# Row gathers of an expert stage issued two pairs ahead, each of four row buffers with its own landing semaphores

## The chip, the cores and the metric

One core of one Trainium2 chip. The metric is the device time of one execution in microseconds (us); the median of several runs is given. The engines are called TensorE (PE in the profile; PEld is its weight load), VectorE (DVE), ScalarE (ACT), GpSimd (POOL) and SyncE (SP).

## The reference, cut to what matters

A model of two layers on 16 sequences of 548 tokens (36 image patches and 512 text rows, width 128): a gated attention, a first mixture of experts, a spiking attention and a second mixture of experts. The change lies in the first mixture of experts, in which each of 32 experts chooses 256 of the 8,768 tokens:

```python
k = min(int(bs * C_CAP) // E, bs)
xf = x.reshape(bs, H)
h = xf @ W_router + b_router
Sm = jax.nn.softmax(h, axis=-1)
G_ek, idx_ek = jax.lax.top_k(Sm.T, k)
tokens = xf[idx_ek]
tok_g = tokens.reshape(NUM_GROUPS, GROUP_SIZE, k, H)
up = jnp.einsum('gjkh,ghf->gjkf', tok_g, W_up) + b_up[:, None, None, :]
act = jax.nn.silu(up).reshape(E, k, D_FF)
Eout = jnp.einsum('ekf,efh->ekh', act, W_down) + b_down[:, None, :]
weighted = G_ek[..., None] * Eout
y = jnp.zeros((bs, H), dtype=x.dtype).at[idx_ek.reshape(-1)].add(weighted.reshape(-1, H))
```

bs is 16 x 548 = 8,768, so k is 274; the width of a hidden row (D_FF) is 341.

## The kernel before, in words

The kernel runs its stages one after the other, each in blocks of its own; a block's engines all finish before the next block begins. The stage of the change is `run_experts` (L1036). Ahead of it `choose_tokens` writes for each expert a list of 320 slots (40 blocks of 8, with room for those that stay empty) to HBM and brings it back as row numbers: `slot_tokens` (`gather_idx`) and `slot_sums` (`scatter_idx`). Behind it `add_rows` (L1190) reads the two copies of the sums from HBM and adds them to the residual H.

The 32 experts are worked in 16 pairs. A pair q has 2 x 320 = 640 slots, five tiles of 128 rows (PTILES = 5); expert o = 0 of the pair owns the first two and a half tiles, o = 1 the rest.

**GpSimd** issues all indirect DMAs. `gather(q)` issues five of them (L1083), each of 128 token rows of 160 floats into `rows[q % 4]`, one of four row buffers. `scatter(q)` issues five (L1092) that add 128 result rows each from `y[q % 2]` to the sums in HBM; ahead of them it waits until the scatter of pair q - 1 has landed (`added`, L1088 to L1089) and hands a y buffer back (`y_free`), and each of the five waits for its y tile (`y_out`, L1091): the first two need expert 0 of the pair, the other three need expert 1. The order on GpSimd is gather(0), then for each q: gather(q + 1), scatter(q).

**TensorE** turns rows (`turn`, L1107: a transpose of each tile, L1113, behind a wait for the gathers of three tiles, `first_in`, or of the last two, `second_in`), multiplies by the up weights (`project_up`, L1122) and by the down weights (`project_down`, L1133, the bias at L1134). The order is written out by hand: turn(q, second part), project_down(q, 0), project_up(q, 1), turn(q + 1, first part), project_down(q, 1), project_up(q + 1, 0), and so on. In particular project_down(q, 1), the last work of pair q, stands behind the wait for the rows of pair q + 1.

**ScalarE** copies the turned rows out of PSUM (L1166, L1168) and applies Silu (L1174). **VectorE** multiplies the down results by the routing weights that came with the rows, and writes y (L1187), behind a wait for `y_done` from TensorE and for `y_free`. **SyncE** loads the up and down weights (L1073, L1076) as TensorE frees their buffers.

Both gathers of neighbouring pairs count on landing semaphores chosen by q % 2, two of them for the first three tiles and two for the last two; TensorE waits for 48 and 32 more at each second pair.

## Time and profile before

| what | value |
|---|---|
| median of 3 runs | 2144.09 us (2139.62 to 2151.6) |
| profiled execution, its own time | 2146.77 us |
| its span, first to last instruction | 2144.9 us |
| PE busy | 1558.1 us (73%) |
| DVE busy | 1316.5 us (61%) |
| ACT busy | 745.3 us (35%) |
| POOL busy | 720.1 us (34%) |
| mean granted TensorE clock | 0.858 of full speed |
| first gather (L1083) to last scatter (L1092) starts | 815.0 to 1094.2 us |

The shares are means over all stages; the stage of the change takes about an eighth of the span. Register, branch, semaphore and DMA-issuing instructions are not counted as busy, except that the indirect DMAs of GpSimd have a duration of their own in the profile, the time in which GpSimd makes their descriptors. "Idle before" is the time in which an engine did nothing before an instruction, with what ended it; "issue" means that the profile shows nothing that it waited for.

### The profile page before, as it was taken

The page shows a single profiled execution, that of the slowest core. Times are in us where ns is not written, and L with a number is a line of the kernel's source. Part 1 is how long each engine was busy: PE and PEld are TensorE (multiplying, and loading weights), DVE is VectorE, ACT ScalarE, POOL GpSimd, SP SyncE. Part 2 cuts the span into 40 slices and gives each one's busy share as a digit, 9 for nine tenths or more (in the row PEclk, how much of TensorE's full clock was granted, in tenths as well). Part 3 has the DMA queues.
Part 4 walks back from the last instruction along what each step waited for, and adds up shares of the span by engine and source line. Part 5 has one row for each costly group of instructions (what it writes and reads, how often), then busy time and mean ns, then how long its engine had stood idle before and what let it go on. Part 6 is the DMA issues. An engine that isn't in the chain of part 4 may idle for free. (4 is left out here: it accounts for less than half of the span.)

```text
span 2144.9 us, 31340 instructions
## 1 busy us (share of the span) xinstructions
PE 1558.1 (73%) x9132; PEld 1091.4 (51%) x9132; DVE 1316.5 (61%) x2105; ACT 745.3 (35%) x1369; POOL 720.1 (34%) x758
## 2 busy tenths in 40 slices
PE   5679999998601006766647548888888758999998
PEld 3457777775301004555534333333333456888787
DVE  3845555555477891111115777877777547989988
ACT  2245555554200002222203346667766321111111
POOL 1345555552000015777754012322221112323322
PEclk8689999999855556888767889999999858999999
DMA  4050000000210002444352000000000000000000
GB/s 136 0 230 1 0 0 0 0 0 0 84 21 0 1 0 60 73 68 77 70 120 66 4 2 2 0 0 0 0 0 0 1 32 7 12 11 15 11 15 14
DMA packets 69696, 60.85 MB, mean 28 GB/s; under 512 B 15789, under 2 KB 63675, under 8 KB 68363
## 3 DMA queue, kind: packets, MB, share of 16 engines
q1 hardware_dynamic: 52174, 47.52, 7.0%
q0 software_dynamic: 15744, 11.85, 3.9%
q10 hardware_dynamic: 1728, 0.85, 0.1%
q8 instruction: 27, 0.44, 0.1%
q14 instruction: 23, 0.19, 0.0%
HBM read 35.06 MB, written 25.18 MB: 28 GB/s over the span
## 5 line engine op out<-in xcount | busy, mean ns | idle before, releaser
L1609 DVE TENSOR_SCALAR at_clip<-at_slot 128x548 bf16<-128x548 f32 (+1 forms) x320 | 226.3, 722 | 79.0 <-PE at_slot L1452 72.2
L1540 ACT ACTIVATE at_clip<-at_slot,at_four 128x548 bf16<-128x548 f32 (+1 forms) x320 | 226.6, 713 | 126.3 <-PE at_slot L1452 124.5
L1452 PE MATMUL at_slot<-at_qm,at_ks 128*128 128x274 bf16 (+1 forms) x1280 | 216.4, 285 | 55.5 <-ACT at_clip L1540 45.4
L1590 POOL TENSOR_SCALAR at_qm<-at_qs,at_headmask 128x548 bf16<-128x548 bf16 x128 | 97.3, 780 | 359.5 <-DVE at_qs L1618 359.5
L1187 DVE TENSOR_SCALAR ex_y<-ex_ps_y,ex_rows 128x128 f32<-128x128 f32 (+1 forms) x96 | 29.2, 346 | 246.5 <-PE ex_ps_y L1134 246.0
L1452 PEld LDWEIGHTS at_slot<-at_qm,at_ks 128*128 128x128 bf16 (+1 forms) x1280 | 90.5, 97 | 150.3 <-ACT at_clip L1540 90.7
L1092 POOL DMA_INDIRECT moe_sums<-ex_y,slot_sums x80 | 125.0, 1563 | 54.4 <-DVE ex_y L1187 32.6
L467 PE MATMUL ga_kv<-ga_kern,ga_v 128*128 128x274 f32 x512 | 132.1, 400 | 14.8 <-ACT ga_kern L552 14.1
L2041 DVE TENSOR_REDUCE mx_routed<-mx_weighted 128x128 f32<-128x1024 f32 x69 | 137.6, 1994 | 2.4
L612 POOL TENSOR_TENSOR ga_rot<-ga_by_cos,ga_by_sin 128x274 f32<-128x274 f32 (+1 forms) x96 | 70.3, 732 | 165.7 <-DVE ga_by_sin L656 165.7
L1133 PE MATMUL ex_ps_y<-ex_down,ex_hid 128*128 128x128 f32 (+3 forms) x576 | 114.1, 357 | 12.5 <-ACT ex_hid L1174 12.5
L80 PE MATMUL mx_e<-ff_expert_out_high,mx_h_E 128*128 128x512 f32 x276 | 110.2, 399 | 10.9 <-DVE mx_weighted L2038 10.8
L467 PEld LDWEIGHTS ga_kv<-ga_kern,ga_v 128*128 128x128 f32 x512 | 92.5, 189 | 40.0 <-ACT ga_kern L552 18.2
L546 ACT ACTIVATE ga_rot<-ga_rot 128x274 f32<-128x274 f32 (+1 forms) x192 | 79.0, 429 | 96.4 <-POOL ga_rot L612 76.6
L1133 PEld LDWEIGHTS ex_ps_y<-ex_down,ex_hid 128*128 128x128 f32 (+3 forms) x576 | 94.6, 230 | 29.8 <-ACT ex_hid L1174 17.2
L82 PE MATMUL mx_e<-ff_expert_out_high,mx_h_E 128*128 128x512 f32 x276 | 108.4, 393 | 0.0
L81 PE MATMUL mx_e<-ff_expert_out_low,mx_h_E 128*128 128x512 f32 x276 | 108.4, 393 | 0.0
L2000 POOL TENSOR_TENSOR mx_h_E<-mx_hid_E,mx_h_E 128x768 fp32r<-128x768 f32 x23 | 43.4, 1885 | 185.5 <-DVE mx_h_E L2031 185.5
L126 PE MATMUL ln_centred<-H,center_sb 128*128 (+1 forms) x256 | 89.3, 483 | 20.7 <-ACTq L168 10.3
L2038 DVE TENSOR_TENSOR mx_weighted<-mx_e,ff_comb 128x512 f32<-128x512 f32 x138 | 88.7, 682 | 9.8 <-PE mx_e L82 6.5
L227 DVE RECIPROCAL ln_rstd<-ln_rstd 128x548 f32<-128x548 f32 x20 | 71.4, 3572 | 34.9 <-ACT ln_rstd L186 34.9
L1974 ACT ACTIVATE mx_silu_E<-mx_a 128x768 f32<-128x768 f32 x23 | 18.7, 814 | 211.8 <-PE mx_b L82 211.8
(346 smaller groups left out, 3798.4 us busy)
## 6 DMA issues: line engine op xcount, KB each, us to landing
moe_sums<-ga_zeros SPq DMA_DIRECT2D x8, 1152.0 KB, 18.9
ar_rows<-moe_sums SPq DMA_DIRECT2D x32, 256.0 KB
ex_down<-in_down SPq DMA_DIRECT2D x32, 192.0 KB, 2.4
out_h<-H SPq DMA_DIRECT2D x22, 192.0 KB, 1.9
H<-in_text SPq DMA_DIRECT2D x1, 4096.0 KB, 20.7
token_rows<-tr_rows SPq DMA_DIRECT2D x16, 256.0 KB
patches<-in_patches SPq DMA_DIRECT2D x1, 1728.0 KB, 7.6
ga_sin<-in_sin SPq DMA_DIRECT2D x1, 1644.0 KB, 10.1
```

The source lines that it names most:

```text
L80: nc.tensor.matmul(out, weights[0], moving[0], start=start, stop=False)
L81: nc.tensor.matmul(out, weights[0], moving[1], start=False, stop=False)
L82: return nc.tensor.matmul(out, weights[1], moving[0], start=False, stop=stop)
L126: nc.tensor.matmul(xc_ps[j][:, 0:HALF], k["center"][:], tokens(H, i, g, j), start=True, stop=True).then_inc(centred, 1)
L467: last = nc.tensor.matmul(kv[:, e, 0:HALF], v[p][:, mt + 2 * side, e * P:(e + 1) * P], kern[g % 2][:, side, :], start=mt == 0 and side == ...
L1092: nc.gpsimd.indirect_dma_start(out=sums, out_offset=bass.IndirectOffsetOnAxis(ap=scatter_idx[:, t, q:q + 1], axis=0), in_=y[q % 2][:, t, : ...
L1133: nc.tensor.matmul(out, hid[o][0:m, f, s0:s0 + n], down[o][0:m, f, :], start=f == 0, stop=False)
L1452: last = nc.tensor.matmul(slot[SLOT[T % 2][u]][0:rows_of(t), s, 0:HALF], ks[p][:, t * P:t * P + rows_of(t)], qm[p][:, h, j * HALF:(j + 1) ...
L1540: nc.scalar.activation(clip[T % 2][u][0:r], slot[SLOT[T % 2][u]][0:r, :, 0:HALF], ACT.Relu, bias=four[0:r], scale=-1.0).then_inc(by_act, 1)
L1590: last = nc.gpsimd.tensor_scalar(qm[p][:, h, :], qs[:], headmask[:, h:h + 1], 1.0, ALU.mult, ALU.mult)
L1609: nc.vector.tensor_scalar(clip[T % 2][u][0:r], slot[SLOT[T % 2][u]][0:r, :, 0:HALF], 4.0, None, ALU.min).then_inc(by_dve, 1)
L2041: nc.vector.tensor_reduce(R[p][t][:], weighted[:].rearrange("p e d -> p d e"), AX.X, ALU.add).then_inc(reduced, 1)
```

## The change

GpSimd issues gather(0) and gather(1) first, and then for each pair q: gather(q + 2), scatter(q). The landing semaphores are four and four, one pair of them for each row buffer (q % 4), and TensorE's counts follow (the fourth part of q in place of the half). The number of DMAs, their sizes, the four row buffers, the two y buffers and TensorE's own order stay as they were.

```diff
@@ -1054,7 +1054,7 @@
-        first_in, second_in = ([sem(f"{n}{p}") for p in range(2)] for n in ("first_in", "second_in"))
+        first_in, second_in = ([sem(f"{n}{p}") for p in range(4)] for n in ("first_in", "second_in"))
@@ -1081,7 +1081,7 @@
-                                                 in_offset=bass.IndirectOffsetOnAxis(ap=gather_idx[:, t, q:q + 1], axis=0)).then_inc(landed[q % 2], 16)
+                                                 in_offset=bass.IndirectOffsetOnAxis(ap=gather_idx[:, t, q:q + 1], axis=0)).then_inc(landed[q % 4], 16)
@@ -1094,9 +1094,10 @@
             gather(0)
+            gather(1)
             for q in range(PAIRS):
-                if q + 1 < PAIRS:
-                    gather(q + 1)
+                if q + 2 < PAIRS:
+                    gather(q + 2)
                 scatter(q)
@@ -1105,9 +1106,9 @@
-                    pe.wait_ge(first_in[r % 2], 48 * nth + 48)
+                    pe.wait_ge(first_in[r], 48 * nth + 48)
                 else:
-                    pe.wait_ge(second_in[r % 2], 32 * nth + 32)
+                    pe.wait_ge(second_in[r], 32 * nth + 32)
@@ -1140,12 +1141,12 @@
             for q in range(PAIRS):
-                turn(q, q % 4, 1, q // 2)
+                turn(q, q % 4, 1, q // 4)
                 project_down(q, 0)
                 project_up(q, 1, q % 2, q // 2 % 2, q // STEP)
                 if q + 1 < PAIRS:
                     n = q + 1
-                    turn(n, n % 4, 0, n // 2)
+                    turn(n, n % 4, 0, n // 4)
```

## Rows read from the trace of the kernel before

**Rows 1.** The page: the span, and one group of its part 5.
```profile
span 2144.9 us, 31340 instructions
...
L1092 POOL DMA_INDIRECT moe_sums<-ex_y,slot_sums x80 | 125.0, 1563 | 54.4 <-DVE ex_y L1187 32.6
```

**Rows 2.** Busy time by stretch (start:end, length; then each engine's busy time, TensorE's clock, DMA).
```profile
845.30:1084.60 239.30, 168.44 (x828) 129.53 (x827) 25.56 (x84) 61.80 (x119) 177.24 (x140) 0.80 0.40 71
...
1096.00:1107.00 11.00, 0.00 (x0) 0.00 (x0) 0.00 (x0) 0.00 (x0) 0.24 (x1) 0.50 0.33 81
```

**Rows 3.** Waits, 815 to 1100 us: engine, line <- releaser: us, times, longest us.
```profile
PE ex_ps_xt L1113 <- DMA ex_rows<-token_rows,slot_tokens: 67.6, 15, 7.4
...
POOL moe_sums L1092 <- DVE ex_y L1187: 32.6, 16, 5.6
...
POOL moe_sums L1092 <- DMA moe_sums<-ex_y,slot_sums: 2.5, 1, 2.5
```

**Rows 4.** Timeline of POOL (start us, us, engine, line, ...), one pair: gathers, then scatters.
```profile
879.50 1.01 POOL L1083 DMA_INDIRECT ex_rows<-token_rows,slot_tokens  x1 [0.30 <-issue]
...
885.85 1.61 POOL L1092 DMA_INDIRECT moe_sums<-ex_y,slot_sums  x1 [0.30 <-issue]
887.77 1.56 POOL L1092 DMA_INDIRECT moe_sums<-ex_y,slot_sums  x1 [0.30 <-issue]
891.02 1.54 POOL L1092 DMA_INDIRECT moe_sums<-ex_y,slot_sums  x1 [1.70 <-DVE ex_y L1187]
...
896.56 1.01 POOL L1083 DMA_INDIRECT ex_rows<-token_rows,slot_tokens  x1 [0.30 <-issue]
```

**Rows 5.** Timeline of all engines, TensorE and VectorE in the same pair.
```profile
884.69 0.90 PE L1113 MATMUL ex_ps_xt<-ident_sb,ex_rows 128*128 128x128 f32 x3 [4.47 <-DMA ex_rows<-token_rows,slot_tokens]
...
890.39 1.00 DVE L1187 TENSOR_SCALAR ex_y<-ex_ps_y,ex_rows 64x128 f32<-64x128 f32 x3 [11.08 <-PE ex_ps_y L1134]
...
896.65 0.86 DVE L1187 TENSOR_SCALAR ex_y<-ex_ps_y,ex_rows 128x128 f32<-128x128 f32 x3 [5.27 <-PE ex_ps_y L1134]
```

**Rows 6.** Waits of POOL, 845.3 to 1084.6 us, the 14 middle pairs.
```profile
POOL moe_sums L1092 <- DVE ex_y L1187: 23.6, 14, 1.8
```

**Rows 7.** Timeline, first pair and last pair: POOL's waits there.
```profile
832.92 1.62 POOL L1092 DMA_INDIRECT moe_sums<-ex_y,slot_sums  x1 [5.63 <-DVE ex_y L1187]
...
839.77 1.54 POOL L1092 DMA_INDIRECT moe_sums<-ex_y,slot_sums  x1 [3.36 <-DVE ex_y L1187]
...
845.31 1.01 POOL L1083 DMA_INDIRECT ex_rows<-token_rows,slot_tokens  x1 [0.30 <-issue]
...
1086.81 1.55 POOL L1092 DMA_INDIRECT moe_sums<-ex_y,slot_sums  x1 [2.52 <-DMA moe_sums<-ex_y,slot_sums]
...
1094.21 1.55 POOL L1092 DMA_INDIRECT moe_sums<-ex_y,slot_sums  x1 [0.31 <-issue]
```

**Rows 8.** Busy time by stretch, TensorE's clock after the wait and later.
```profile
884.70:890.10 5.40, 5.40 (x24) 4.67 (x25) 0.00 (x0) 1.77 (x2) 4.02 (x3) 0.50 0.31 48
890.10:895.50 5.40, 3.78 (x23) 2.93 (x22) 0.97 (x3) 2.90 (x5) 3.87 (x3) 0.97 0.47 68
```

**Rows 9.** DMA issues, 815 to 1100 us: count, median us from issue to landing.
```profile
ex_rows<-token_rows,slot_tokens POOLq DMA_INDIRECT x80, 2.6
moe_sums<-ex_y,slot_sums POOLq DMA_INDIRECT x80, 3.3
```

**Rows 10.** Timeline, TensorE in the first pair (clock 0.50).
```profile
820.20 0.90 PE L1113 MATMUL ex_ps_xt<-ident_sb,ex_rows 128*128 128x128 f32 x3 [7.39 <-DMA ex_rows<-token_rows,slot_tokens]
823.10 3.54 PE L1122 MATMUL ex_ps_up<-ex_xt,ex_up 128*128 128x320 f32 x6 [1.99 <-issue]
826.43 0.63 PE L1113 MATMUL ex_ps_xt<-ident_sb,ex_rows 128*128 128x128 f32 x2
827.43 1.65 PE L1133 MATMUL ex_ps_y<-ex_down,ex_hid 128*128 128x128 f32 x6 [0.37 <-ACT ex_hid L1174]
...
832.19 1.44 PE L1122 MATMUL ex_ps_up<-ex_xt,ex_up 128*128 128x320 f32 x2
```

## The prediction, made before the changed kernel was run

> **What bounds the kernel now.** The page comes first: a span of 2144.9 us, and among its groups the scatters of the expert stage, 80 instructions of 1563 ns on GpSimd [rows 1]. The blocks run one after the other, so what matters is which engine paces this stage, and whether its end passes on to what follows. The table of busy time by stretch gives the stage's middle, 14 pairs in 239.3 us, so 17.09 us each: GpSimd is busy for 177.24 us, TensorE for 168.44. The next block begins only after the stage: nothing but its first 0.24 us on GpSimd runs in the 11 us behind it [rows 2]. So a shorter stage is a shorter kernel, us for us.
>
> The table of waits is the trap of this stage. It shows TensorE waiting 67.6 us for gathered rows in 15 waits, and GpSimd waiting only 32.6 us for VectorE's y tiles and 2.5 us for a scatter to land [rows 3]. The timeline says which wait costs. GpSimd issues without a pause except for one: five gathers from 879.50 to 885.85, 6.35 us, then five scatters from 885.85 to 896.56, 10.71 us, with a wait of 1.70 us ahead of the third [rows 4]. An ordinary gap between two DMA issues is 0.30 us, so 1.40 us is waiting and 15.66 of the 17.06 us is issue work. TensorE has a period without its wait of 17.09 - 4.47 = 12.6 us. GpSimd is the pacer.
>
> Where the 1.40 us comes from: gather(q + 1) is issued directly ahead of scatter(q). TensorE begins to turn its rows at 884.69, that is 5.2 us after the first gather's start and 1.2 us before scatter(q) begins; only behind that turn does it do the second down product of pair q, whose y tiles VectorE starts at 890.39 [rows 5]. The third scatter of pair q wanted them at 887.77 + 1.56 + 0.30 = 889.6, and got the first at about 890.7. The landing is late by a hair, each pair, because a result of pair q stands behind rows of pair q + 1.
>
> **The change, part by part.** *Three-deep order.* gather(q + 2) is now ahead of scatter(q). TensorE's turn that releases the second down product of pair q waits for gather(q + 1), which was issued ahead of scatter(q - 1), one GpSimd period earlier. With scatter(q - 1) as zero, those rows are turned at -1.2, y of pair q is whole at about -1.2 + 5.7 + 1.0 = +5.5, and its third scatter is reached at 15.66 + 3.8 = 19.4. There are 14 us to spare, so the wait goes. Over the 14 middle pairs it is 23.6 us [rows 6], of which 14 x 0.30 = 4.2 us is the ordinary gap: **19.4 us off**.
>
> *One gather moves into a pause that exists.* After its first ten gathers GpSimd waits 5.63 us until 832.92 for y of the first pair, and 3.36 us more until 839.77 for its second half [rows 7]. Gather(2) now stands there: it begins at 832.92 - 5.63 + 0.30 = 827.6 and takes 6.35 us, so the first scatter starts at 833.9, 1.0 us late. The second is done by 837.4, still 2.3 us before the third can start, whose time TensorE sets with rows of pair 1 that are no later than before. So the first scatter group ends where it did, at 845.3, and 13 gathers follow in place of 14: **6.35 us off**.
>
> *The end has two bare landing waits.* scatter(q) first waits for scatter(q - 1) to land, 3.3 us from its last issue [rows 9]. Six microseconds of gathers hide that, except ahead of scatter(15), which waits 2.52 us [rows 7]. Now neither scatter(14) nor scatter(15) has gathers ahead of it: 2.52 - 0.30 = **2.2 us on**. The bounds are 0 and 3.3; I take the row of the same step.
>
> *y buffers.* VectorE may write y of pair q + 1 once scatter(q) begins; before, y came after that anyway. Now TensorE is early and VectorE waits for it, starts at the beginning of scatter(q) and is wanted a whole period later. Behind it wait TensorE's two PSUM buffers of y, which let it go one expert of each kind ahead. Nothing of this reaches GpSimd.
>
> *Row buffers and weights.* gather(q + 2) fills the buffer of pair q - 2, whose last reader was done before scatter(q - 2) ended, and no wait is added. SyncE's weight loads go by TensorE's progress, as before. The four more semaphores, TensorE's waits on them and the changed counts add no instruction to the loop: 0, and at most the 0.3 us of one gap each at the block's ends.
>
> *The DMA queue.* Gathers land 2.6 us after issue [rows 9] and are issued 6.35 / 5 = 1.27 us apart, so two or three are in flight. The order has more of them ahead in pairs, not in time: the issue rate is nearly unchanged, and ten in a row at the start are nothing new. I price it at 0; if each scatter group lost the 0.07 us by which a first instruction of a group is longer (1.61 against 1.54), it would be 1 us.
>
> The sum: -19.4 - 6.35 + 2.2 = **-23.6 us**. The profiled execution took 2146.77 us, 1.9 over its span, and should take 2123.2; the median of the runs shown is 2144.09, 2.7 lower than that execution, and gives **2120.5 us**, 1.1% less.
>
> What the larger wait would say: if TensorE's 67.6 us [rows 3] were the bound, the sum would be 2076. GpSimd's 15.66 us of issue per pair forbids it, and TensorE will go on waiting, about 15.7 - 12.6 = 3 us per pair, since it runs out of rows. The Trainium skill, "Perfetto Trace Analysis", section "Optimization Strategies", says to keep the matmul engine busy and to work on whatever it waits for. Read as a count of TensorE's idle time it would give 2076; read as a search for the blocking engine it leads to the same place as the rows.
>
> **The rivals.**
>
> *1. TensorE paces part of the stage (within 0.5%).* Its period is 12.6 us only with a mixed clock. After its wait it ran at a granted 0.50, the lower level (1.2 GHz), and from 890.1 at 0.97, the higher (2.4 GHz) [rows 8]. With its waits moved, more of its work may fall at the lower level. At 16.4 us a pair, GpSimd waits 0.7 us again, and the gather saved at the front is waited away: 14 x 0.7 = 10 us off, 2134.5. Against it: between 12.6 and 15.66 nothing shows. 6 in 100.
>
> *2. TensorE stays at the lower level (slower).* The place is the stage's first pair, at a granted 0.50 for most of it: turning takes 0.90 and 0.63, an up product 3.54, a down product 832.19 - 827.43 = 4.76 [rows 10]. A pair is 0.90 + 0.63 + 2 x 3.54 + 2 x 4.76 = 18.1 us. It decides from 17.09 us on; at 18.1 the 14 pairs cost 14.2 us more: 2158.3. Against it: an engine that never waits is what the rows show at the higher level, and this one would never wait. 3 in 100.
>
> The Trainium skill, "TensorE: Matmul & The Clock Gate", section "What's actually happening", has the array at half rate by default and at full rate once it is active. By that rule a TensorE that paces the stage would get the full rate back, the time of rival 2 could not last, and the sum stays 2120.5; the change from 0.50 to 0.97 in the rows agrees.
>
> *3. The extra distance does nothing (within 0.5%).* Some order that I overlook, as ScalarE's wait for the down product before last, keeps y of pair q behind the newest gather. Then the waits stay, gather(2) still hides at the front, and the end costs 2.2: -4.2, so 2139.9. For it: TensorE's hand-written order and the two-deep buffers of y and the turned rows are unchanged. Against it: the slack of 14 us just worked out. 5 in 100.
>
> **How the numbers follow.** A change of 0.5%, 10.7 us, is about what a measurement of this kernel can tell from none. The forecast has 86 in 100; a hundredth of it falls under the bound, the runs shown being spread over 12 us. Faster 0.85, within 0.5% 0.12 (6 + 5 + 1), slower 0.03. The forecast's own range: from the price bounds, 2.1 less (1.1 by the landing wait, 1 by the queue) to 2.2 more gain, and the run spread of about 4.5 below and 7.5 above the median give 2113 to 2129. It reaches into rivals no further than 2132, as those hold 14 in 100 together: 2112 to 2132.
>
> **What would show each step.** GpSimd's period between first gathers falls from 17.06 to 15.7 us. Its waits for y fall from 32.6 to some 2.3 us, all at the third scatter; its waits for a landing become two of 2.5 us. The first scatter starts at 833.9 and the fourth gather group at 845.3. TensorE still waits for rows, 3 us a pair. The last scatter starts at about 1070.6. I am wrong if y waits remain past the first pair, if the scatters' mean moves from 1563 ns, if TensorE has no wait left, or if time comes back in another stage.

## The result, and the profile after

| what | before | changed |
|---|---|---|
| median of 6 runs each, same comparison | 2145.2 us (2139.62 to 2155.33) | 2131.86 us (2128.85 to 2134.52) |
| ratio, 95% interval | | 0.9931 (0.9916 to 0.9946) |
| profiled execution, its own time | 2146.77 us | 2130.16 us |
| mean granted TensorE clock | 0.858 | 0.862 |

The ratio times 2145.2 is 14.8 us less, with 18.0 and 11.6 as the interval's ends. The sum had said 23.6 less. The change is faster, by more than 0.5%, and by less than the sum said.

The page of the changed kernel: its span, and the scatters. Lines from L1098 on are one higher than before, so VectorE's y is L1188 and the down product L1134.

```profile
span 2128.3 us, 31340 instructions
...
L1092 POOL DMA_INDIRECT moe_sums<-ex_y,slot_sums x80 | 124.8, 1560 | 34.6 <-issue 21.3
```

Against [rows 1] the scatters are as long (1560 against 1563 ns), and the idle time ahead of them fell from 54.4 to 34.6 us. VectorE's y no longer heads the list; what is left is mostly the ordinary 0.30 us between two issues. Busy time by stretch, in the middle of the stage:

```profile
850.20:1044.80 194.60, 141.88 (x775) 107.92 (x775) 23.87 (x79) 58.73 (x114) 156.47 (x125) 0.89 0.46 81
```

GpSimd is busy for 156.47 of 194.6 us, 80%, against 177.24 of 239.3, 74%, in [rows 2]. The waits of the stage (us, times, longest):

```profile
PE ex_ps_xt L1114 <- DMA ex_rows<-token_rows,slot_tokens: 33.9, 9, 7.4
...
POOL moe_sums L1092 <- DVE ex_y L1188: 10.8, 9, 3.5
...
POOL moe_sums L1092 <- DMA moe_sums<-ex_y,slot_sums: 2.5, 1, 2.5
```

TensorE waits half as long for rows as in [rows 3] (this trace lacks about a quarter of the landing records, so some of its waits may be missing), and GpSimd's waits for y fell from 32.6 to 10.8 us. Where they are is on GpSimd's timeline, over the whole stage:

```profile
844.76 1.54 POOL L1092 DMA_INDIRECT moe_sums<-ex_y,slot_sums  x1 [2.93 <-DVE ex_y L1188]
...
850.29 1.01 POOL L1083 DMA_INDIRECT ex_rows<-token_rows,slot_tokens  x1 [0.30 <-issue]
...
860.45 1.54 POOL L1092 DMA_INDIRECT moe_sums<-ex_y,slot_sums  x1 [0.30 <-issue]
...
865.99 1.00 POOL L1083 DMA_INDIRECT ex_rows<-token_rows,slot_tokens  x1 [0.30 <-issue]
...
1056.46 1.54 POOL L1092 DMA_INDIRECT moe_sums<-ex_y,slot_sums  x1 [2.58 <-DVE ex_y L1188]
...
1067.86 1.54 POOL L1092 DMA_INDIRECT moe_sums<-ex_y,slot_sums  x1 [2.45 <-DMA moe_sums<-ex_y,slot_sums]
...
1075.24 1.54 POOL L1092 DMA_INDIRECT moe_sums<-ex_y,slot_sums  x1 [0.30 <-issue]
```

A period of the middle is 865.99 - 850.29 = 15.70 us, and its third scatter (860.45) begins after an ordinary gap, where [rows 4] had 1.70. The two landing waits ahead of the last two scatter groups are there, 2.58 and 2.45 us (the first, at 1056.46, is put down to VectorE, whose y of that pair was long made). But the first pair has two waits for y, 2.93 us (at 844.76) and, in the next view, 3.45 us, where the forecast had one of 2.3. The fourth gather group begins at 850.29, that is 33.9 us after the first gather; the forecast had 30.3. The timeline of the first pair in the trace of the changed kernel:

```profile
828.85 0.93 PE L1134 MATMUL ex_ps_y<-ex_down,ex_hid 128*128 128x128 f32 x6 [0.73 <-ACT ex_hid L1175]
...
830.56 0.87 PE L1134 MATMUL ex_ps_y<-ex_down,ex_hid 128*64 128x128 f32 x6
...
833.95 0.95 POOL L1083 DMA_INDIRECT ex_rows<-token_rows,slot_tokens  x1 [0.30 <-issue]
837.72 0.86 DVE L1188 TENSOR_SCALAR ex_y<-ex_ps_y,ex_rows 128x128 f32<-128x128 f32 x3 [22.46 <-remote]
...
837.86 1.35 ACT L1175 ACTIVATE ex_hid<-ex_ps_up,cols_sb 128x320 f32<-128x320 f32 x3 [8.78 <-remote]
838.35 1.62 POOL L1092 DMA_INDIRECT moe_sums<-ex_y,slot_sums  x1 [3.45 <-DVE ex_y L1188]
```

TensorE ended the down product of the first three tiles at about 830.56 + 0.87 = 831.4. VectorE, idle and with nothing else to wait for, began its y only at 837.72, some 6 us later; ScalarE went on at 837.86. Both started about 2.8 us after the end of the last of the 15 gathers (834.90). The profile names no releaser here but "remote"; the trace's list of semaphore updates says more. TensorE's own update for the finished product, the one that VectorE waits for, stands in it 21.31 us after the first gather's start, 6.2 us after the modelled end of the last matmul; those of the next up product and of the next turn stand there too, within 0.2 us of it, and VectorE starts 0.03 us behind. So it is TensorE's signals that came late, and not VectorE that was slow to start; in the traces without this, the same update stands 0.01 us after the last matmul. What held the signals back is not shown. Below this is called the pause.

The end of the stage is not visible in the waits. The last scatter begins at 1094.21 [rows 7] in the kernel before and the first load of the next stage (SyncE, L1211, now L1212) at 1102.26, 8.05 us later; here it is:

```profile
1084.90 0.38 SPq L1212 DMA_DIRECT2D ar_rows<-moe_sums  x1
```

1084.90 - 1075.24 = 9.66 us, 1.6 us more. The instructions of GpSimd's queue at the block's last line show where. Behind the landing of the last scatter stands a DRAIN, with which GpSimd ends the block; first in the kernel before, then in the changed one:

```profile
L1041 POOLq DRAIN  x1: 3804/3804/3804, 1097.8 to 1097.8; - x1
...
L1041 POOLq DRAIN  x1: 5437/5437/5437, 1078.8 to 1078.8; - x1
```

It takes 3.80 us before and 5.44 us in the changed kernel, and that is the 1.6 us.

### The profile page after: what moved, and what is told of

It reads as the page before. It is cut to its first block and busy times, and to the rows that moved or that the text cites. A ratio compares the mean times of both kernels' runs of the same rounds, so it can differ in the third digit from the quotient of the medians.

```text
span 2128.3 us, 31340 instructions
## 1 busy us (share of the span) xinstructions
PE 1544.4 (73%) x9132; PEld 1081.9 (51%) x9132; DVE 1318.0 (62%) x2105; ACT 744.3 (35%) x1369; POOL 719.1 (34%) x758
## 5 line engine op out<-in xcount | busy, mean ns | idle before, releaser
L1453 PE MATMUL at_slot<-at_qm,at_ks 128*128 128x274 bf16 (+1 forms) x1280 | 216.9, 285 | 55.2 <-ACT at_clip L1541 45.7
L1188 DVE TENSOR_SCALAR ex_y<-ex_ps_y,ex_rows 128x128 f32<-128x128 f32 (+1 forms) x96 | 29.2, 346 | 216.2 <-PE ex_ps_y L1135 106.0
L1092 POOL DMA_INDIRECT moe_sums<-ex_y,slot_sums x80 | 124.8, 1560 | 34.6 <-issue 21.3
L1134 PE MATMUL ex_ps_y<-ex_down,ex_hid 128*128 128x128 f32 (+3 forms) x576 | 99.7, 325 | 34.3 <-ACT ex_hid L1175 22.2
L1134 PEld LDWEIGHTS ex_ps_y<-ex_down,ex_hid 128*128 128x128 f32 (+3 forms) x576 | 82.6, 204 | 49.1 <-ACT ex_hid L1175 26.9
L2039 DVE TENSOR_TENSOR mx_weighted<-mx_e,ff_comb 128x512 f32<-128x512 f32 x138 | 88.8, 684 | 10.3 <-PE mx_e L82 7.0
L1975 ACT ACTIVATE mx_silu_E<-mx_a 128x768 f32<-128x768 f32 x23 | 18.7, 814 | 212.5 <-PE mx_b L82 212.5
```

The lines of the kernel that those rows point to most:

```text
L1092: nc.gpsimd.indirect_dma_start(out=sums, out_offset=bass.IndirectOffsetOnAxis(ap=scatter_idx[:, t, q:q + 1], axis=0), in_=y[q % 2][:, t, : ...
L1134: nc.tensor.matmul(out, hid[o][0:m, f, s0:s0 + n], down[o][0:m, f, :], start=f == 0, stop=False)
L1453: last = nc.tensor.matmul(slot[SLOT[T % 2][u]][0:rows_of(t), s, 0:HALF], ks[p][:, t * P:t * P + rows_of(t)], qm[p][:, h, j * HALF:(j + 1) ...
L2039: nc.vector.tensor_tensor(weighted[:, 4 * a:4 * a + 4, :], e_ps[a][:].rearrange("p (e d) -> p e d", e=4), by, ALU.mult).then_inc(weighed, 1)
```

## The experiments

To compare traces I take five marks: the start of the first scatter, of the third, and of the sixth (pair 1) after the first gather's start; the same for the last scatter; and the gap from there to the first load of the next stage. Stage and gap together are what the rest of the kernel sees. What follows the gap took 1039.6 to 1047.0 us in these traces, though no edit touches it: between traces the marks say more than the spans.

| kernel | 1st scatter | 3rd | 6th | period | last | gap | last + gap |
|---|---|---|---|---|---|---|---|
| before | 17.93 | 24.78 | 36.68 | 17.10 | 279.22 | 8.05 | 287.3 |
| changed | 21.97 | 28.38 | 40.26 | 15.69 | 258.86 | 9.66 | 268.5 |
| changed, again | 18.82 | 24.77 | 36.65 | 15.69 | 255.33 | 9.51 | 264.8 |
| split head | 17.88 | 24.73 | 36.75 | 15.69 | 255.39 | 9.49 | 264.9 |
| three pairs ahead | 25.06 | 28.86 | 40.76 | 15.69 | 255.48 | 10.56 | 266.0 |
| semaphores only | 15.66 | 20.82 | 32.70 | 16.80 | 271.99 | 10.41 | 282.4 |
| before, a | 17.86 | 23.22 | 35.10 | 16.92 | 275.58 | 8.02 | 283.6 |
| before, b | 17.81 | 23.17 | 35.05 | 16.91 | 275.46 | 7.91 | 283.4 |
| split tail | 18.87 | 22.66 | 34.56 | 15.71 | 251.48 | 9.60 | 261.1 |
| old order, filler | 17.89 | 26.28 | 38.16 | 15.84 | 263.62 | 8.07 | 271.7 |
| warm head, split tail | 22.00 | 28.28 | 40.16 | 15.69 | 256.77 | 9.47 | 266.2 |
| six semaphores, split tail | 22.03 | 28.45 | 40.32 | 15.69 | 256.95 | 9.45 | 266.4 |
| gather(2) late | 16.38 | 21.54 | 39.71 | 15.71 | 258.46 | 9.45 | 267.9 |
| warm, head and tail split | 19.10 | 25.49 | 37.51 | 15.72 | 254.55 | 9.53 | 264.1 |

Each number is a difference of two starts in a kernel's timeline; the period is the mean of the eleven behind the sixth scatter.

### The changed kernel, traced again

The kernel is unedited.

> The changed kernel once more, unedited. In its first trace the stage from first gather to last scatter start took 258.9 us (before: 279.2), which is 3.2 us longer than forecast; the first scatter started 22.0 us after the first gather (before: 17.9), although TensorE's first down product had ended 6.2 us before VectorE could start on it. Theory A (a long run of gathers holds back the completion signals of the engines): the same pause of some 6 us is there again, first scatter at about +22, fourth gather group at +33.9, and the time is 13 to 17 us under the kernel before. Theory B (the pause is chance of one execution): no pause, first scatter at +18.9, fourth gather group at +30.3, last scatter at +255.6, time about 20 us or more under the kernel before.

2127.18 us (2125.3 to 2129.34), ratio 0.9924 (0.9911 to 0.9938): 16.3 us less. In the first pair of this trace:

```profile
830.39 1.54 PE L1134 MATMUL ex_ps_y<-ex_down,ex_hid 128*64 128x128 f32 x6
...
832.08 0.86 DVE L1188 TENSOR_SCALAR ex_y<-ex_ps_y,ex_rows 128x128 f32<-128x128 f32 x3 [18.42 <-PE ex_ps_y L1135]
...
833.60 1.62 POOL L1092 DMA_INDIRECT moe_sums<-ex_y,slot_sums  x1 [0.30 <-issue]
...
839.55 1.54 POOL L1092 DMA_INDIRECT moe_sums<-ex_y,slot_sums  x1 [2.46 <-DVE ex_y L1188]
```

VectorE starts 0.15 us after TensorE's last long down product ends (830.39 + 1.54 = 831.93). GpSimd has issued its gathers by then and scatters without a wait; the one wait is 2.46 us at the third scatter. The fourth gather group began at +30.3 and the last scatter at +255.33, where the forecast had +30.3 and 1070.6 - 815.0 = +255.6. So this trace is the forecast (theory B of the expectation), and the pause, which puts the last scatter 3.5 us later, is something that some executions have and others don't. The waits of GpSimd in the middle, 851.4 to 1050 us:

```profile
POOL moe_sums L1092 <- DVE ex_y L1188: 2.4, 8, 0.3
```

Eight waits with a sum of 2.4 us, and none over 0.3: these are ordinary gaps. The step of the forecast that takes the waits away can be read in one pair, and at the lower clock at that:

```profile
897.32 0.90 PE L1114 MATMUL ex_ps_xt<-ident_sb,ex_rows 128*128 128x128 f32 x3 [3.34 <-DMA ex_rows<-token_rows,slot_tokens]
...
903.02 1.00 DVE L1188 TENSOR_SCALAR ex_y<-ex_ps_y,ex_rows 64x128 f32<-64x128 f32 x3 [8.38 <-PE ex_ps_y L1135]
...
917.99 1.55 POOL L1092 DMA_INDIRECT moe_sums<-ex_y,slot_sums  x1 [0.30 <-issue]
```

```profile
897.60:903.00 5.40, 5.40 (x25) 4.67 (x25) 0.00 (x0) 0.49 (x1) 4.48 (x4) 0.50 0.36 53
```

TensorE waits 3.34 us for rows, turns them and does the down product at a granted 0.50, as in [rows 8]. But this y belongs to the next scatter group (the third scatter of the group then running had started at 902.30, after an ordinary gap): it is whole at 904.0, and its third scatter starts at 917.99, so 14 us are to spare, as the forecast had worked out. The new order takes the wait away by itself, though the product is as slow as before.

### Head split finer, and one pair further ahead

```diff
             gather(0)
             gather(1)
-            for q in range(PAIRS):
+            gather(2, range(3))
+            scatter(0, range(2))
+            gather(2, range(3, PTILES))
+            scatter(0, range(2, PTILES))
+            for q in range(1, PAIRS):
```

> Third gather group cut in two: three of its five DMAs ahead of the first scatter, two between its second and third DMA, where GpSimd waits for VectorE anyway. Theory A (run of 15 gathers holds back completion signals): 13 gathers in a row in place of 15 end 2.5 us earlier, so VectorE starts on the first y about 2.5 to 4 us earlier than in the changed kernel and the stage is 2 to 4 us shorter, 2128 to 2130. Theory B (chance, or a delay that has nothing to do with the gathers): as the changed kernel within 1 us, since the gather group was hidden in both.

2129.25 us, ratio 0.9933 (0.9917 to 0.9948), no different from the changed kernel. Its trace has no pause, so it decides nothing on theory A. The first scatter came 0.9 us sooner, at 17.88, and the third at the same 24.73: TensorE and VectorE set that one. Scattering two tiles sooner gives nothing if the third must wait.

```diff
             gather(0)
             gather(1)
+            gather(2)
             for q in range(PAIRS):
-                if q + 2 < PAIRS:
-                    gather(q + 2)
+                if q + 3 < PAIRS:
+                    gather(q + 3)
```

> Gathers three pairs ahead, 20 gathers ahead of the first scatter. GpSimd's issue work is the same, its waits for y in the middle were gone already. By issue work alone the first scatter can start at 20 x 1.25 = +25.1, its group is not held any more and ends at +34.5, where the fourth gather group has been issued already: 12 more gather groups follow. Against the changed kernel's +33.9 with 13 groups: 0.6 later, one group of 6.3 us less, and one more bare landing wait of 2.2: 3.5 us faster than the changed kernel (theory B). Theory A: the signals of TensorE are held until the last of the 20 gathers has landed, about +28, then the second expert's chain of 6.4 us sets the third scatter at about +35, and the group ends at +40.5: 2.5 us slower than the changed kernel.

2128.31 us, ratio 0.9933 (0.9916 to 0.995), and the last scatter at 255.48. The 3.5 us expected were against the trace with the pause, whose last scatter came at 258.86, and there they are (3.4). Against the trace without it (255.33) a further pair ahead gave nothing, though it leaves 12 gather groups behind the sixth scatter instead of 13. The head had no room for it: twenty gathers in a row put the first scatter at 25.06 and the sixth at 40.76, 4.1 us later than in the trace above, and a third bare wait for a landing came at the end. The gap was 10.56. There was no pause: TensorE's signal stands 0.01 us after the down product, with twenty gathers in a row.

### The semaphores alone

The order of before with the changed kernel's eight landing semaphores:

```diff
             gather(0)
-            gather(1)
             for q in range(PAIRS):
-                if q + 2 < PAIRS:
-                    gather(q + 2)
+                if q + 1 < PAIRS:
+                    gather(q + 1)
                 scatter(q)
```

> The order of the kernel before (one pair ahead) with the eight landing semaphores of the change. Theory A and theory B alike: within 1 us of the kernel before, all landing waits and the periods of 17.1 us as there. A rival (the semaphores themselves cost, at the block's start or end, as the 1.6 us more between last scatter and first load of the next stage suggest): 1 to 3 us slower than before.

2144.51 us (10 runs), ratio 1.0009 (0.9996 to 1.0022). The semaphores alone change nothing in time that can be told (the interval allows 0.9 us less to 4.7 more), and they bring no gain: the gain is the order's. In its trace the waits of GpSimd for y, 848 to 1080 us, are those of the old order:

```profile
POOL moe_sums L1092 <- DVE ex_y L1187: 20.6, 14, 1.8
```

The gap, though, was 10.41 us, 2.4 more than in the trace of before (GpSimd's DRAIN took 6.25 us in place of 3.80), and the stage was 7 us shorter than there. Two effects that cancel, or a trace of before that was a long one: that called for more traces of before.

### The kernel before, traced twice more

Both kernels are unedited.

> The kernel before, unedited, for a second trace. In the runs so far a kernel of the old order (with eight semaphores) had a stage of 272.0 us against 279.2 in the first trace of before, its first scatter at +15.7 against +17.9 us, with the first down product at 0.93 us per six matmuls in place of 1.65. Theory C (the stage before has several lengths, set by TensorE's clock in its first pairs, and the forecast was made from a long one): stage between 270 and 280 us, first scatter at +15.7 or +17.9 by the clock of that moment. Theory D (the eight semaphores make the difference): 279 and +17.9 again. The drain of GpSimd behind the last scatter, 3.8 us here against 5.4 in the changed kernel and 6.3 with eight semaphores in the old order: by its count of semaphores 3.8 again, by chance another value.

> The kernel before once more, a third trace of it. Theory C: another stage length between 270 and 280 us. Theory D: 279 us. Drain behind the last scatter: 3.8 us if it belongs to the kernel, something else if to chance.

One run each: 2145.37 and 2149.03 us. The last scatter began at +275.58 and +275.46, against +279.22 in the trace that the forecast rests on. GpSimd's waits for y in the middle of the first of them:

```profile
POOL moe_sums L1092 <- DVE ex_y L1187: 22.0, 14, 1.7
```

In the second it is 21.8 us; [rows 6] has 23.6. And in the first pair of the first of them:

```profile
839.60 1.54 POOL L1092 DMA_INDIRECT moe_sums<-ex_y,slot_sums  x1 [1.87 <-DVE ex_y L1187]
```

1.87 us of waiting for the second half of y, where [rows 7] has 3.36. In both traces a stage of before is 3.7 us shorter than the one I summed against. The executions' own times don't say so, because the rest of the kernel was longer in these: in the first by 816.38 - 814.99 = 1.4 us ahead of the stage and 1.0 behind it, in the second by 2.5 and 3.8.

### The tail split

The last five gathers are spread over the last two turns of the loop, so that something hides part of each landing.

```diff
-                if q + 2 < PAIRS:
+                if q + 2 < PAIRS - 1:
                     gather(q + 2)
+                elif q + 2 < PAIRS:
+                    gather(q + 2, range(3))
+                elif q + 1 < PAIRS:
+                    gather(q + 1, range(3, PTILES))
                 scatter(q)
```

> The changed kernel, but the last gather group (pair 15) cut: three DMAs ahead of scatter(13) as before, its last two ahead of scatter(14). They fill the pause of 2.6 us in which GpSimd waits for scatter(13) to land, and TensorE's first part of pair 15 needs only the first three. If the tail is a bare landing wait: one wait of 2.5 us gone, stage 2.2 us shorter than the changed kernel (last scatter at about +253.1 against +255.3). If the two late DMAs hold up y of pair 15: the wait comes back at the first scatter of pair 15, and nothing is gained.

2121.72 us (2120.42 to 2126.24), ratio 0.9903 (0.9885 to 0.9922), 20.8 us less than before (0.0097 of 2143.22). The end of the stage on GpSimd's timeline:

```profile
1044.02 1.01 POOL L1083 DMA_INDIRECT ex_rows<-token_rows,slot_tokens  x1 [0.30 <-issue]
...
1046.63 1.61 POOL L1092 DMA_INDIRECT moe_sums<-ex_y,slot_sums  x1 [0.30 <-issue]
...
1058.26 1.55 POOL L1092 DMA_INDIRECT moe_sums<-ex_y,slot_sums  x1 [2.55 <-DMA moe_sums<-ex_y,slot_sums]
...
1065.67 1.55 POOL L1092 DMA_INDIRECT moe_sums<-ex_y,slot_sums  x1 [0.30 <-issue]
```

Two gathers in front of scatter(14) hide its landing wait (0.30 at 1046.63), and only scatter(15) waits, 2.55. From the sixth to the last scatter it took 251.48 - 34.56 = 216.9 us, against 218.7 in the changed kernel's second trace: 1.8 us. Its head had no pause, and a third scatter 2.1 us sooner than there: TensorE had the higher clock in the first down product.

```profile
826.55 0.94 PE L1138 MATMUL ex_ps_y<-ex_down,ex_hid 128*128 128x128 f32 x6 [0.58 <-ACT ex_hid L1179]
...
833.06 1.62 POOL L1092 DMA_INDIRECT moe_sums<-ex_y,slot_sums  x1 [0.30 <-issue]
```

A tile's six matmuls take 0.94 us instead of the 1.65 of [rows 10]. So the tail explains 1.8 of its lead, and a head that varies by execution the rest. That the version is faster than before is measured; that it is faster than the changed kernel rests on the 1.8 us in the traces, since 0.9903 and 0.9924 have intervals that overlap.

### The old order with TensorE kept busy

Kernel before, with sixteen matmuls whose result nothing reads, where TensorE otherwise waits for rows:

```diff
                 if q + 1 < PAIRS:
+                    for _ in range(16):
+                        nc.tensor.matmul(fill_ps[:], k["ones_bf"][:], k["down_b3"][:, 0:512], start=True, stop=True)
                     n = q + 1
                     turn(n, n % 4, 0, n // 2)
```

> The kernel before (one pair ahead) with 16 matmuls of 512 bf16 columns, whose results nobody reads, ahead of each turn that waits for gathered rows; they take some 3.5 us of TensorE's 4.5 us wait. Theory C in its stronger form (GpSimd waits 1.4 us a pair because TensorE does the second down product at the lower clock after its wait, 4.8 us in place of 2.7): the clock stays at the higher level, y is there 2.1 us earlier, the 14 waits go without any change of the gathers' order, period 15.7 us, time 2124 to 2129. Theory E (only the order of the gathers can take the wait away, since the down product stands behind the newest rows): the waits stay, period 16.5 to 17.1 us, time within 5 us of the kernel before.

2133.09 us (2130.34 to 2137.81), ratio 0.9952 (0.9933 to 0.9971): 10.3 us less, by adding work, where theory C had 14 to 19. Its timeline in one pair:

```profile
912.07 3.40 PE L1149 MATMUL ex_ps_fill<-down_b,ones_bf 128*128 128x512 bf16 x15
...
917.73 0.55 PE L1114 MATMUL ex_ps_xt<-ident_sb,ex_rows 128*128 128x128 f32 x3 [2.26 <-DMA ex_rows<-token_rows,slot_tokens]
...
918.21 0.87 PE L1134 MATMUL ex_ps_y<-ex_down,ex_hid 128*64 128x128 f32 x6
...
920.88 1.00 DVE L1190 TENSOR_SCALAR ex_y<-ex_ps_y,ex_rows 64x128 f32<-64x128 f32 x3 [9.78 <-PE ex_ps_y L1135]
...
922.72 1.55 POOL L1093 DMA_INDIRECT moe_sums<-ex_y,slot_sums  x1 [0.30 <-issue]
```

TensorE still waits 2.26 us for the rows (917.73), then does the down product in 920.88 - 918.21 = 2.7 us. In the kernel before it began at 885.52:

```profile
885.52 1.54 PE L1133 MATMUL ex_ps_y<-ex_down,ex_hid 128*64 128x128 f32 x6
```

and VectorE at 890.39 [rows 5], 4.9 us later. TensorE's clock in that place, with the filler:

```profile
917.60:923.00 5.40, 5.00 (x32) 3.83 (x32) 0.96 (x3) 1.81 (x4) 4.42 (x4) 1.00 0.38 79
```

1.00 where [rows 8] has 0.50. The second y tile group is there before GpSimd gets to it. Its waits, 855.7 to 1074 us:

```profile
POOL moe_sums L1093 <- DVE ex_y L1190: 6.6, 13, 1.3
```

6.6 us in 13 waits, of which 13 x 0.30 = 3.9 are gaps; the period fell to 15.84. The order of the gathers was the same as before. So GpSimd's wait of 1.40 us a pair needed two things: the down product stood behind the newest rows, and it ran at the lower clock because TensorE had just waited for those rows. Taking away the first removes the wait (the pair shown above, at 0.50); taking away the second removes most of it. From the sixth to the last scatter it took 225.5 us against 240.5 in the first of the two traces of before above, 15 us less, but the head lost 3.1: the third scatter came at 26.28 against 23.22 and 23.17. In the first pair TensorE had no wait to fill there, and the fillers took 3.4 us ahead of its second down product. Hence 10.3 us and not 14 or more. This was not in my prediction, which gave the order as the cause and had the clock only as a danger for afterwards.

### Is it the clock that brings the pause?

In the changed kernel's first trace, the one with the pause, the first down product ran faster (0.87 us for its third tile) than in its second, without (1.54). Three kernels on the changed order look at this, and at the two other things that could bring the pause. Fourteen filler matmuls ahead of TensorE's first turn, with the split tail:

```diff
+            for _ in range(14):
+                nc.tensor.matmul(fill_ps[:], k["ones_bf"][:], k["down_b3"][:, 0:512], start=True, stop=True)
             turn(0, 0, 0, 0)
             project_up(0, 0, 0, 0, 0)
```

> The kernel of the cut last gather group, and 14 matmuls of 512 bf16 columns with a result that nobody reads ahead of TensorE's first turn, where it waits 7.4 us for the first rows. Theory C (the head's length is TensorE's clock in its first two pairs): the first down product at 0.93 us per six matmuls in every execution, the third scatter at +22.7 us with no wait, the group's end at +34.6, as the e7 trace had by luck; stage +251.5, and the median 1 to 2 us under e7's. Rival (the clock of the head is no matter, or the extra matmuls make the first turn late): third scatter at +24.8 or later, median equal to e7's or above.

2128.54 us, ratio 0.9926 (0.9912 to 0.9939). The first down product ended at +14.0, 1.1 us sooner than in the changed kernel's first trace, and VectorE began 7.4 us after it:

```profile
832.65 0.95 POOL L1084 DMA_INDIRECT ex_rows<-token_rows,slot_tokens  x1 [0.30 <-issue]
836.45 0.86 DVE L1195 TENSOR_SCALAR ex_y<-ex_ps_y,ex_rows 128x128 f32<-128x128 f32 x3 [22.49 <-remote]
```

Again VectorE starts 2.8 us after the end of the last gather (832.65 + 0.95 = 833.60), and the time won on TensorE is lost. The expectation missed: the third scatter came at 28.28 and not 22.7, and the median is above that of the split tail alone (2121.72), though the intervals of the two ratios overlap.

Six landing semaphores in place of eight, with the split tail:

```diff
-        first_in, second_in = ([sem(f"{n}{p}") for p in range(4)] for n in ("first_in", "second_in"))
+        first_in, second_in = ([sem(f"{n}{p}") for p in range(3)] for n in ("first_in", "second_in"))
```

> The kernel of the cut last gather group with three landing semaphores for the first tiles and three for the last (pair number modulo 3), six in place of eight. If GpSimd's drain at the block's end grows with the landing semaphores (3.8 us with four, 5.4 with eight): about 4.6 us, and 0.8 us less in all. If it goes by something else in the program: 3.8, 5.4 or 6.3 us, with no order in it. The stage itself as in e7, last scatter at +251.5 or +253.6 by the head's clock.

2128.87 us, ratio 0.9928 (0.9911 to 0.9946). There was a pause of 6.3 us, without any filler, and a gap of 9.45 us as with eight (the DRAIN took 5.36 us; eight gave 5.44 and 6.25). Neither follows the number of semaphores alone. This kernel differs from the split tail in nothing but those semaphores, and its median is 7 us higher (their ratios' intervals overlap); 5.3 us of that is what last scatter and gap differ by in the two traces, most of it the pause.

Gather(2) behind the first scatter group, so that only ten gathers run in a row:

```diff
             gather(0)
             gather(1)
-            for q in range(PAIRS):
+            scatter(0)
+            gather(2)
+            for q in range(1, PAIRS):
```

> The changed kernel with the third gather group behind the first scatter group in place of ahead of it: everything later is two pairs ahead as before. It measures the term of 6.35 us by itself. If the group was hidden in GpSimd's wait for the first y: first scatter at +17.9 (or +15.7), third at +24.8 (or +20.8), first scatter of pair 1 at +43.0 (or +39.0) against +36.7 in the changed kernel at the same clock, stage 4.3 to 6.4 us longer, 2131 to 2134. If it was not hidden: stage and time as the changed kernel.

2133.83 us, ratio 0.9948 (0.9931 to 0.9966). There was no pause, and the first scatters ran early:

```profile
834.38 1.62 POOL L1092 DMA_INDIRECT moe_sums<-ex_y,slot_sums  x1 [4.10 <-DVE ex_y L1190]
...
845.08 1.01 POOL L1083 DMA_INDIRECT ex_rows<-token_rows,slot_tokens  x1 [0.30 <-issue]
...
857.71 1.62 POOL L1092 DMA_INDIRECT moe_sums<-ex_y,slot_sums  x1 [0.30 <-issue]
```

But the five gathers now stand between the fifth scatter and the sixth: from the third scatter to the sixth it took 18.17 us against 11.88, 6.29 us more. That is the term of 6.35 us for the gather that moves into the first wait, measured by itself.

### Head and tail split, TensorE warm

The split tail and the fourteen fillers, both as above, and a head with thirteen gathers before the first scatter, of which the edit is:

```diff
             gather(0)
             gather(1)
-            for q in range(PAIRS):
+            gather(2, range(3))
+            scatter(0, range(2))
+            gather(2, range(3, PTILES))
+            scatter(0, range(2, PTILES))
+            for q in range(1, PAIRS):
```

> The kernel with warmed TensorE and cut last gather group (e9), and the third gather group cut in two as in e2: three of its DMAs ahead of the first scatter, two between the second and third scatter. In the traces of the changed kernel, e9 and e10 VectorE and ScalarE started 6.2 to 7.4 us late on TensorE's first down product; in those TensorE had done it at the higher clock while 15 gathers stood ahead of the first scatter. If the 15 gathers in a row make the pause at that clock: 13 end 2.5 us earlier, the pause is gone or 2.5 us shorter, first scatter at +16.6 to +19.5, stage 251.5 to 254.5, time 2121 to 2126. If the pause goes with the execution (as the missing landing records of these traces suggest) and not with the number of gathers: the pause is there at full length in a trace that lacks landing records and absent in one that has them, first scatter +22 or +16.6.

2123.88 us (2119.68 to 2125.92), ratio 0.9907 (0.9891 to 0.9924): 19.9 us less than before.

```profile
829.36 0.95 POOL L1084 DMA_INDIRECT ex_rows<-token_rows,slot_tokens  x1 [0.30 <-issue]
...
832.72 0.86 DVE L1199 TENSOR_SCALAR ex_y<-ex_ps_y,ex_rows 128x128 f32<-128x128 f32 x3 [19.59 <-remote]
...
832.86 1.35 ACT L1186 ACTIVATE ex_hid<-ex_ps_up,cols_sb 128x320 f32<-128x320 f32 x3 [6.68 <-remote]
```

VectorE starts 2.4 us after the end of the thirteenth gather (829.36 + 0.95 = 830.31). Against the run of fifteen above, VectorE's start came 2.9 us sooner after the first gather (832.72 - 814.25 = 18.5, against 836.45 - 815.08 = 21.4), and two gathers are 2 x 1.25 = 2.5 us. So in these two traces the pause ends with the run of gathers and 2.4 to 2.9 us behind it. That is a rule for where it ends and not for when it is there: the second trace of the changed kernel and that of the split tail have the same run of fifteen and no pause, the split tail's with TensorE at the higher clock.

## Why the prediction was right, and where its size was off

The time (2131.86) is inside the range of 2112 to 2132 by 0.14 us, with runs that spread over 5.7: that it lies inside is luck, since the middle of the forecast, 2120.5, was missed by 11.4. The second comparison (2127.18) is well inside. The sign, the case that I held likeliest and the mechanism came true; the size did not. Step by step:

- **GpSimd is the pacer.** Right. The period went from 17.10 to 15.69 us, where the forecast had 15.7. It was 15.69 to 15.72 in every version of the new order, with TensorE at 0.84 to 0.91 of full speed between 855 and 1040 us.
- **19.4 us of waits in the middle go.** Right in kind: what is left of them is gaps, and the 14 us to spare were measured. The size was that of one execution. Two other traces have 22.0 and 21.8 us in place of 23.6.
- **6.35 us for the gather in the first wait.** Right: 6.29 when it was put back behind the first scatter group. Without the pause it was hidden in full, and the fourth gather group began at +30.3 as forecast.
- **2.2 us on for a second landing wait.** Right: 2.58 and 2.45 us for the two, and splitting the tail took 1.6 to 2.1 us off in four traces.
- **The scatters' length and the queue, 0.** Right: 1560 ns, and in the second trace of the changed kernel rows landed 2.6 and sums 3.3 us after issue, as in [rows 9].
- **TensorE goes on waiting.** Right: 43.9 us in 12 waits in the second trace; without the first one of 7.4 it is 3.3 us each, where 3 was forecast. The Trainium skill, "Perfetto Trace Analysis", section "Optimization Strategies", wants the engines optimized that keep the matmul engine idle. The rows agree that this engine was GpSimd, and show that TensorE's own idle time gives no size for the gain: 67.6 us of waiting fell by 23.7 in that trace, and 16.3 us came off the kernel.
- **Four more semaphores, at most 0.3 us at the block's ends.** Wrong. The gap behind the last scatter was 7.9 to 8.1 us in the four traces with the old order and four semaphores; it is 9.4 to 9.7 with the changed order, and 10.4 and 10.6 with the semaphores alone and with three pairs ahead. That is some 1.5 us that the sum did not have. It is GpSimd's DRAIN at the end of the block: 3.80 us in those four, 5.36 to 5.44 with the changed order, 6.25 in the other two.
- **So the first scatter group ends where it did.** Right in some executions, wrong in others: 3.6 us late with the pause (+33.9 against +30.3).
- **The range.** Its own terms (2.1 and 2.2 us, and a spread of 4.5 and 7.5) give 2113.8 to 2130.1, where it says 2113 to 2129; and rival 1's 2134.5 leaves out the 2.2 us of the end.

**Where the 23.6 went.** In the second trace of the changed kernel the last scatter began 279.22 - 255.33 = 23.9 us earlier than in the trace that I summed against. That trace's stage was 3.7 us longer than two others of the same kernel: 20.2 is left. The gap takes 1.5 back, which is 283.5 (the mean of a and b in the table's last column) - 264.8 = 18.7. With the pause it is 283.5 - 268.5 = 15.0. Measured were 14.8 (11.6 to 18.0) and 16.3 (13.3 to 19.1); the intervals hold both values. The step that failed is therefore one of bookkeeping first: I set one profiled execution's stage against a median of whole kernels, and took off the 2.7 us by which that execution was over the median without asking in which stage they were. Then it is the price of 0 to 0.3 us for the block's end, which measured 1.5, and where the pause is there, the 3.6 us for which the sum has no term.

None of the rivals came. TensorE did not pace the stage: its clock in the middle went up, from 0.80 to 0.85 in one trace and 0.89 in the other, not down. Against rival 2 the forecast said that the rows show an engine that never waits at the higher level; [rows 8] show TensorE busy for 5.40 of 5.40 us at 0.50 and for 3.78 of 5.40 at 0.97, so they don't say that, and TensorE went on waiting, so no run tries it. And the extra distance did something. But rival 1 had hold of the part that I had left out: the clock after TensorE's wait had its part in y's lateness. The order was enough to cure it at the lower clock, and the clock cured most of it in the old order: filling TensorE's wait with matmuls that nothing reads gave 10.3 us. The Trainium skill, "TensorE: Matmul & The Clock Gate", section "HAM oscillation — how this bites in real kernels", tells of a matmul loop that starts each step at the lower rate after waiting for a DMA, and advises to restructure such a loop so that the array stays at the higher one. The traces agree that the work behind such a wait ran at the lower rate (0.50 in [rows 8]) and at the higher one with the wait filled (1.00), with one thing beside it: what came off was not TensorE's time but another engine's wait.

**What stays open.** What brings the pause. It was there in four traces of the fourteen, all with 13 or 15 gathers in a row and with TensorE at the higher clock in the first down product; the split tail's trace had both and no pause, and the three with 13, 15 and 20 in a row at the lower clock had none. The same four traces, and the one with gather(2) late, hold about 4,420 to 4,730 records of DMA landings where the others hold some 5,890, so that the profile can give no median landing there, and about 11,000 semaphore updates where the others hold 12,500. Whether the profiler's own load has a part in the pause was not tried, and so how often it is in the timed runs is not known either. Open too is what makes the DRAIN at the block's end longer: it grew with eight semaphores and the old order, and with six and the new, and four semaphores with the new order weren't tried. It goes with the program and not with the execution, being 3.80 us in three traces of the kernel before and 5.44 in both of the changed one.

**The version to take** is the split tail (2121.72) or the one with head and tail split and a warm TensorE (2123.88); both are nearly 1% faster than the kernel before. Their difference can't be told from none, and I take the first, which adds no work. Its 2121.72 comes with a trace without the pause; the two kernels that share its tail and had the pause measured 2128.54 and 2128.87, so part of its lead may be chance.

## What to carry to other kernels

Look for the engine that issues without pause and for the one wait in its period; the gain is that wait and not the much larger one of the engine that it feeds, and issuing further ahead pays only while there are waits to put the work into (three pairs ahead gave nothing over two). When a result comes late by a hair behind a wait, look at the granted clock behind that wait as well as at the order, since either may cure it. Before a saving in one stage is set against a median of whole runs, measure that stage in more than one trace of the kernel before, and look at what stands between the stage's last instruction and the next one's first.

## What the runs showed of the hardware that was not expected

- TensorE's semaphore updates can come late while GpSimd issues indirect DMAs: in the four traces with the pause they stand 4.1 to 7.3 us after the matmuls, and VectorE started at once upon them, 2.4 to 2.9 us after the last of 13 or 15 gathers in a row had ended. In the other ten traces the update stands 0.01 us after the last matmul; six of these have ten gathers in a row, four have 13 to 20.
- The same end of a block took 7.9 to 10.6 us from its last scatter's start to the next block's first load, by the kernel's order and semaphores. What differs is the length of GpSimd's DRAIN: 3.80, 5.36, 5.44 or 6.25 us, and the same in every trace of the same kernel.
- Sixteen matmuls that nothing reads, placed in a DMA wait, took the down product that followed from 4.9 to 2.7 us and shortened the kernel by 10.3 us.
